# Starting layer 0's gathers on a partly built table, and moving half of its one-hots to ScalarE, in a graph network on one core

## The reference

```python
xt = jnp.einsum('ni,rio->rno', x, weight)            # 8 relations, 6250 x 256 each
messages = xt[edge_type, dst]                        # one row of 256 for each edge
out = segment_sum(messages, src, 6250)               # summed by src
x = layernorm(x + relu(out + bias))
```

## Time and profile before

| | us |
|---|---|
| median of 3 runs | 6381.3 (6370.28 to 6396.28) |
| span of the profiled execution | 6384.2 |
| edges loaded, first tiles of the table, block 0 ranked | 0 to 124 |
| slots 0 to 223 beside the rest of the table | 124 to 431 |
| sums | 431 to 2976, first add at 439.3 |
| second layer's tables | 2976 to 3100 |
| walk | 3100 to 5950 |
| final stage | 5950 to 6384 |

### The profile page before, as it was taken

The page is one execution under the profiler, slowest core; times in us unless marked ns, Lnnn a source line. Parts: engine busy times, 40 slices in busy tenths (PEclk is TensorE's granted clock), DMA queues, the critical chain, the costliest instruction groups (busy, mean ns, idle before and its releaser), DMA issues. The chain is left out here.

```text
span 6384.2 us, 87308 instructions
## 1 busy us (share of the span) xinstructions
PE 4813.9 (75%) x20011; PEld 3228.2 (51%) x20011; DVE 4590.7 (72%) x14055; ACT 2915.4 (46%) x7582; POOL 3197.8 (50%) x3370
## 2 busy tenths in 40 slices
PE   8986666666666666557777777877777777788898
PEld 4543334333333333334566665666666666666666
DVE  6977777777777777556377777777777777777766
ACT  4764444444444444002355555555555555555322
POOL 2025565555656566665255555555555555554000
PEclk9997787787777878678889988899899989889999
DMA  6432222222222222335455555555555555555100
GB/s 192 138 120 82 83 85 82 83 83 81 84 83 83 83 84 84 107 91 175 140 156 166 161 161 162 157 168 162 162 161 163 165 162 168 157 162 154 52 11 28
DMA packets 346029, 779.02 MB, mean 122 GB/s; under 512 B 75122, under 2 KB 176519, under 8 KB 345525
## 3 DMA queue, kind: packets, MB, share of 16 engines
q0 software_dynamic: 214608, 659.52, 35.5%
q1 hardware_dynamic: 127285, 111.00, 5.6%
q10 hardware_dynamic: 3632, 2.88, 0.2%
HBM read 691.52 MB, written 81.59 MB: 121 GB/s over the span
## 5 line engine op out<-in xcount | busy, mean ns | idle before, releaser
L1719 POOL DMA_INDIRECT big<-kv_table,walk_s x1664 | 1578.5, 949 | 1246.9 <-PE pb L1758 601.7
L757 POOL DMA_INDIRECT big<-xt_table,big x1617 | 1542.3, 954 | 1044.6 <-issue 504.0
L932 PE MATMUL pb<-big,walk_s 128*128 128x256 f32 x3234 | 1285.1, 494 | 457.9 <-DVE node_a L1143 200.4
L766 ACT ACTIVATE walk_s<-walk_s,big 128x128 f16<-128x128 f16 x3136 | 1076.9, 393 | 1197.4 <-DVE walk_s L1065 656.7
L1143 DVE TENSOR_TENSOR node_a<-node_a,pb 128x256 f32 (+1 forms) x1617 | 667.0, 413 | 680.2 <-remote 369.2
L1758 PE MATMUL pb<-big,early 128*128 128x264 f32 x3328 | 1000.5, 450 | 188.2 <-issue 169.9
L932 PEld LDWEIGHTS pb<-big,walk_s 128*128 128x128 f32 x3234 | 650.8, 246 | 628.5 <-issue 526.3
L1894 DVE TENSOR_TENSOR big<-big,pb 128x1024 f32<-128x1024 f32 x416 | 505.7, 1216 | 573.0 <-PE pb L1742 287.8
L1742 PE MATMUL pb<-node_a,late 128*128 x3328 | 869.7, 407 | 20.5 <-ACT late L1821 13.6
L1758 PEld LDWEIGHTS pb<-big,early 128*128 128x128 f32 x3328 | 698.3, 221 | 362.3 <-issue 223.9
L843 PE MATMUL pb<-walk_s 128*128 128x256 f16 x1568 | 501.2, 322 | 420.9 <-ACT walk_s L766 272.4
(11 more groups left out here) (313 smaller groups left out, 5743.8 us busy)
## 6 DMA issues: line engine op xcount, KB each, us to landing
xt_table<-big SPq DMA_DIRECT2D x98, 512.0 KB
big<-kv_table,walk_s POOLq DMA_INDIRECT x1664
big<-xt_table,big POOLq DMA_INDIRECT x1617
late<-pen_table SPq DMA_DIRECT2D x832, 12.1 KB
kv_table<-big SPq DMA_DIRECT2D x49, 256.0 KB
x_store<-big SPq DMA_DIRECT2D x49, 128.0 KB
big<-in_x POOLq DMA_DIRECT2D x48, 128.0 KB, 3.3
big<-x_store SPq DMA_DIRECT2D x6, 1024.0 KB, 11.9
```

The costliest lines, as they stand in the source:

```text
L757: e.indirect_dma_start(sum_rows[:, q % SUM_ROWS, k, :], None, xt_table, bass.IndirectOffsetOnAxis(ap=idx_all[:, i:i + 1], axis=0))\
L766: ins = e.activation(hot_v[:, t % SORT_HOTS, v, :], hot_q[:, t % SORT_HOTS, :], ACT.Copy, scale=part_c[:, t:t + 1])
L932: e.matmul(pb[:, bank, 0:D], one_hot, sum_rows[:, q % SUM_ROWS, k, :], start=True, stop=True)\
L1719: e.indirect_dma_start(rows[:, q % ROW_RING, k, 0:2 * D], None, kv_table, bass.IndirectOffsetOnAxis(ap=src_i[:, i:i + 1], axis=0))\
```

## The change

The rows of `xt_table` stand by node, then by relation, so that a store writes pieces of 4 KB, and the low nodes of all relations stand first in it. Since the edges come sorted by `dst`, a block's gathers touch only the tiles of its own nodes.

The l0 stage makes only products 20 to 83 (`TABLED` 84) ahead of the sums. Slots 0 to 143 (`AHEAD`) are put between products 56 and 84. The remaining 112 products run inside the sums, one after every sixth item up to item 666, in bank 1, one at a time (`product_at`); each waits until the one before it is copied out. The turns of their tiles run there too (`turn_at`). ScalarE takes the copy at the end of the same item.

GpSimd's gathers of a block wait for the stores of as many tiles as the block can touch (`tiles_for`, 19 for block 0). The remaining 80 slots of the lead are made up in items 0 to 79, which carry two slots each (`lead`). Block 1 is ranked in 54 slots as before. Blocks 2 to 12 are ranked in 126 slots each, all with the scan in PSUM. A scalar flag tells whether `dst` really is sorted and a block's last nodes lie within its tiles; if not, the kernel takes a branch that makes the whole table first, which these inputs don't take.

The one-hots of every second quad of items come from ScalarE: four activations `Abs(place - iota)` into bf16, 128 columns each, and one `Relu(1 - ...)` over 512 columns.

Three smaller things: the loads of x for tiles 7 to 48 move from GpSimd's queue to SP's; the bias copies into the sums move ahead of the slots; an iota of 128 x 1664 (`walk_iotas`, L1321) moves from the first stage to the place behind GpSimd's last gather.

```diff
-        xt_v = xt_table.rearrange("(r n) o -> n r o", r=REL)
+        xt_v = xt_table.rearrange("(n r) o -> n r o", r=REL)
+AHEAD = BT + 16
+FIRST, BEHIND, TABLED = 4 * EARLY + 36, 2, 4 * EARLY + 64
+TABLE_PACE = 6
+        def hot_by_scalar(i):
+            return i < T and i // QUAD % 2 == 1
+        def lead(i):
+            return min(AHEAD + 2 * i, PRE + i)
+        def slots_at(i):
+            return range(lead(i), lead(i + 1))
+        def product_at(i):
+            n = TABLED + i // TABLE_PACE
+            return n if i % TABLE_PACE == 0 and n < 4 * W else None
+        def tiles_for(b):
+            if b == 0:
+                return TABLED // 4 - 2
+            first = b * BT - (W - 1)
+            return min(W, (TABLED + (first - 30) // TABLE_PACE) // 4)
...
+            with e.Else():
+                e.sem_inc(s_sorted, 1)
+                for i in range(PART_ITEMS):
+                    b = block_of(i)
+                    if i == 0 or b != block_of(i - 1):
+                        e.wait_ge(s_xst[0], 16 * tiles_for(b))
+                        e.wait_ge(s_xst[1], 16 * tiles_for(b))
+                    gather(e, i, tiles_for(b))
@@ l0_scalar @@
+            for n in range(4 * EARLY, TABLED):
+                if n % 4 == 0:
+                    keep_x(e, n // 4 + 1)
+                keep_product(e, n)
...
+                for t in slots_after(n):
+                    slot(t)
+            quad_abs(QUAD)
+            for i in range(ITEMS):
+                for t in slots_at(i):
+                    slot(t)
+                if turn_at(i) is not None:
+                    keep_x(e, turn_at(i))
+                if product_at(i) is not None:
+                    keep_product(e, product_at(i))
+                if hot_by_scalar(i + 1) and (i + 1) % QUAD == 0:
+                    quad_relu((i + 1) // QUAD)
+                if hot_by_scalar(i + QUAD + 1):
+                    quad_abs(i + QUAD + 1)
@@ l0_tensor @@
             for i in range(ITEMS):
-                slot(PRE + i)
+                for t in slots_at(i):
+                    slot(t)
...
                 total(i)
+                if turn_at(i) is not None:
+                    turn_x(e, turn_at(i))
+                if product_at(i) is not None:
+                    product(e, product_at(i))
@@ l0_vector @@
             for i in range(ITEMS):
                 j = closing(i)
-                if j is None or j >= READY:
+                if not hot_by_scalar(i) and (j is None or j >= READY):
```

More of the change, by code:

```diff
@@ L527, in edges_float @@
             e.memset(raw_next[:, last], JUNK).then_inc(s_padded, 1)
+            c = Chain(e, s_dv0)
+            for b in range(PART_BLOCKS):
+                c.add(e.memset(limits[:, b:b + 1], P * tiles_for(b)))
             e.wait_ge(s_rawload, 16 * 12)
@@ L740, in table_io, with gather @@
         def table_io(e):
-            for n in range(2 * EARLY, 2 * W):
-                store_xt(e, n)
+            for w in range(EARLY, W):
+                if w + 2 < W:
+                    load_x(e, w + 2)
+                store_xt(e, 2 * w)
+                store_xt(e, 2 * w + 1)
+        def gather(e, i, tiles):
+            q, k = divmod(i, 4)
+            if i < T:
+                got.done(e, block_of(i))
+            else:
+                e.wait_ge(s_close, LISTED)
+            if k == 0 and q >= SUM_ROWS:
+                summed.done(e, (q - SUM_ROWS) * 4 + 3)
+            e.indirect_dma_start(sum_rows[:, q % SUM_ROWS, k, :], None, xt_table[0:tiles * P * REL, :],
+                                 bass.IndirectOffsetOnAxis(ap=idx_all[:, i:i + 1], axis=0))\
+                .then_inc(s_rows[q % SUM_ROWS], 16)
@@ new lines, in part_gather @@
+        def part_gather(e):
+            e.wait_ge(s_flag, 1)
+            flag = e.value_load(unsorted[0:1, 0:1], min_val=0, max_val=1)
+            with e.If(flag == 1):
+                order_move(e)
+                e.sem_inc(s_sorted, 1)
+                for i in range(PART_ITEMS):
+                    gather(e, i, W)
+            with e.Else():
+                e.sem_inc(s_sorted, 1)
+                for i in range(PART_ITEMS):
+                    b = block_of(i)
[3 more added lines that the diff above has]
+                    gather(e, i, tiles_for(b))
@@ L744, in l0_gather @@
         def l0_gather(e):
-            for w in range(EARLY + 2, W):
-                load_x(e, w)
             e.wait_ge(s_xst[0], 16 * W)
             e.wait_ge(s_xst[1], 16 * W)
[L749 to L759, removed]
+            for i in range(PART_ITEMS, ITEMS):
+                gather(e, i, W)
@@ L883, in slot @@
                     close_place()
[L884 to L885 removed]
+                for b, s in ranking(t):
+                    if b == 1 and s == 13:
                         counts(b)
[L887 removed]
+                    if s == (23 if b == 1 else 1):
                         windows(b)
[L889 removed]
+                    if s == (49 if b == 1 else 115):
                         turn_pos(b)
+                    if s == (111 if b == 1 else 121) and b + 1 < BLOCKS:
+                        counts(b + 1)
             turn_x(e, EARLY)
[L893 to L907 removed]
+            for n in range(4 * EARLY, TABLED):
+                if n % 4 == 0:
+                    turn_x(e, n // 4 + 1)
+                    e.wait_ge(s_xtc, n // 4 + 1)
+                product(e, n)
+                for t in slots_after(n - BEHIND):
+                    slot(t)
+                if n == 4 * EARLY + 7:
+                    counts(0)
+                if n == 4 * EARLY + 12:
+                    windows(0)
+                if n == 4 * EARLY + 33:
+                    turn_pos(0)
+            for n in range(TABLED - BEHIND, TABLED):
                 for t in slots_after(n):
@@ L1146, in l0_vector @@
             e.memset(x_in[:, 2, :], 0.0).then_inc(s_xz, 1)
+            c.add(e.memset(ones_p, 1.0))
             c.add(e.memset(cum_w[:, 0, :], 0.0))
```

258 lines of the change are left out of this document (161 added, 97 removed).

## The result

The changed kernel takes 6439.0 us (median of 6 runs, 6414.3 to 6470.1) against 6380.0 (6 runs, 6370.3 to 6407.3): a ratio of 1.0085, 95% interval 1.0059 to 1.011. It is slower, by more than 0.5%. I had forecast 6334, faster, with a range of 6255 to 6435; the time lies 4 us above the range and on the other side of the kernel before, where the rival of the lock step had it.

A forecast was written before the change was run, and what follows sets the result against it. Non-overlapping stages: TensorE's products and slots bound the first; in the sums no engine is full, and work plus stops set the pace. -171 + 51 + 71 + 1 = -48: 6336 on the profile, 6334 on the median, range 6255 to 6435.

The forecast's parts named there:

- the rival of the lock step: Items 80 to 672: TensorE and ScalarE wait for each other around products, pace 1.95, +213 us; time 6475, chance 0.19.
- Start of the gathers: Stage before the sums: first gather at 260, first add at 268 in place of 439.3, -171 us.
- The first 80 items: Start of the sums, two slots an item: 191 us in place of 140, +51, between +36 and +70.
- Products in items 80 to 672: Sums, a product every sixth item: 1.71 us an item against 1.59, over 592 items +71 us.
- about 1.4 us of idle TensorE with the semaphores: Sums, at each product: TensorE's next slot waits while ScalarE copies the product (0.59) and then scales that slot (0.66).
- stops: Sums: time in which several engines stand at once, of unknown cause; 0.36 us of an item's 1.59.
- the 0.36: Sums: us per item left between the modelled work of 1.23 and the pace of 1.59, added as a constant.
- ScalarE's one-hots: Sums, every second quad: 0.26 us an item more on ScalarE, expected to change nothing; 0, at most -20 us.
- 1.06 is below the pace: nothing: Sums: ScalarE's 0.70 us an item plus 0.26 for one-hots and 0.10 for copies, expected to cost no time.
- The stops shrink: Rival, sums: a gather's rows lie close together, so 0.36 us falls by a quarter, -145 us; time 6190, chance 0.05.
- The clock rule: Rival, items 80 to 672: products raise TensorE's clock to 0.89, +18 in place of +71; time 6283, chance 0.09.
- The last part: Behind the sums: the moved iota of 9.15 us hides behind waits for the adds, +1 us, +9 if uncovered.

The follow-up runs named there:

- the first experiment: The changed kernel, with ScalarE's product copies in the sums four items later (turned tiles' copies one later, their turns two later): 6288.7 us, ratio 0.9838 to the kernel before.
- Experiment 4: The changed kernel, but VectorE makes the one-hots of every quad of the sums and ScalarE none: 6352.2 us, ratio 0.9955 to the kernel before.
- experiment 5: The changed kernel with the copies four items later and all one-hots of the sums on VectorE: 6313.5 us, ratio 0.9834 to the kernel before.
- experiment 9: The changed kernel with copies four items later and the sums' products and copies cut from 512 columns to 32: 6258.3 us, ratio 0.9789 to the kernel before.
- experiments 8 and 10: Changed kernel, copies four items later, plus TensorE's slots one item later (6294.8 us, 0.9798), or instead adds two items behind, not three (6360.2 us, 0.9941).

## Why the prediction was wrong

- **Start of the gathers:** right, and by the mechanism that the sum had. First gather 255.5 for 260, first add 263.6 for 268. ScalarE is the fullest engine from 200 to 256 (53.74 of 56 us), the nineteen tiles were stored well before, and the list came last.
- **The first 80 items:** +40.7 for +51, right in kind. With the copies later they take 162.9 us in place of 180.0 (426.93 less 264.04), so some 17 us of it were already the tie.
- **Products in items 80 to 672:** this step failed, +191 for +71. The term that was mis-sized is "about 1.4 us of idle TensorE with the semaphores": TensorE stood 3.0 us behind ScalarE's scalings for each product (257.7/85), and ScalarE 4.9 us ahead of its copy, for a product of 1.72. With 3.0 in its place the forecast's own sum gives an estimate of 1.94 us for an item, where 1.92 was measured; with no such idle time it gives 1.69, as in the first experiment. That 1.94 comes out so well is in part luck, as some of the 3.0 are stops, which the 0.36 counts again. And this is what was wrong in kind: I had added the stops as a constant 0.36 to an item's work. A pause at a product was no longer shared by engines with prepared work; it held all that stood behind the copy.

The experiments show how the parts of this step hang together. These are the us from the add of item 80 to that of item 672 (944.1 in the kernel before):

| | as changed | short products and copies | all one-hots on VectorE |
|---|---|---|---|
| copy in its own item | 1135.1 | 1024.2 | 1050.1 |
| copy four items later | 1001.7 | 963.2 | 995.8 |

Taking the tie away first gives 133 us, then the products' and copies' work 38, and 19 are left unassigned. Taking the work away first gives 111 us, and the tie then 61. So the shares depend on the order: behind the tie the same work costs three times what it costs without it, and the one-hots 85 us in place of 6.

- **The rival that came true:** lock step, 6475 forecast for a span of 6468.4, decided by a pace above 1.84, measured 1.92. That the two times lie so close is partly luck: its products were to cost +213 and cost +191, and 33 us that it didn't have came in behind the sums. I had given it 0.19, and argued against it that "VectorE's own chain hides part of each". It hid what the earlier trace rows shows as slack of ScalarE behind VectorE; a wait of 4.9 us every six items uses that up. That TensorE then falls to the low clock is seen at 1005.49, but the clock in the mean rose (below), so that part of the rival isn't what costs the time.
- **ScalarE's one-hots:** "1.06 is below the pace: nothing" was wrong in this kernel, and right without the tie. All of them on VectorE saves 0.013 of the ratio, some 83 us, with the tie, and nothing that can be measured without it; from item 672 on, where there is no copy, the pace is 1.56 us in both kernels. The Trainium skill, "ScalarE: Activation LUTs", Rules for kernel authors, advises VectorE and not ScalarE for relu, max, min, add and mul. Experiment 4 agrees, where ScalarE is late; experiment 5 shows no cost where it isn't.
- **The stops shrink:** no. 1471.0 against 1477.1 us after item 672, with the rows of a gather close together.
- **The clock rule:** the granted clock did rise with the products, 0.83 against 0.79, and to between 0.85 and 0.89 in the experiments with whole products; with short ones it was 0.79 and 0.80. The Trainium skill, "TensorE: Matmul & The Clock Gate", Part 1, says that activity releases the throttle; the trace agrees in direction. The pace followed the waits and not the clock: in experiment 4 the clock is 0.89 at a pace of 1.78, in experiment 9 it is 0.80 at 1.63.
- **The last part:** +1 forecast for the iota. It takes 9.18 us at 3023.86, and the last record gathers still wait 6.53 us for the adds, so it is hidden. The +34 us of the table lie behind the sums, in unchanged code; the twelve profiles of this case have 3384 to 3429 us there. The profiled run is also 31 us above its kernel's median, while the medians are 59 us apart. I take it for the spread of single executions; no run was made for it.
- **A reading:** VectorE's share from 200 to 431 is 196.24/231, 85% and not 86%. Nothing rests on it.

What the stops are stays open. So does whether four items' delay is better than one.

The version with the copies four items later beats both kernels: 0.9838 (0.9781 to 0.9896) against the kernel before, 91 us by the medians on the same chip, where my sum for the change as written had been 48.

## What to carry to other kernels

Put an instruction that waits for another engine's long result where that result is surely there, some items later in the in-order queue, and not in the item that asks for it: what is lost isn't the wait but all prepared work queued behind it. When you cost a wait, ask which engine was ahead before and by how much; an engine whose idle time is all "behind X" is ahead of the others, and an edit that turns that into idle time behind something else makes its whole work count, the cheap parts too: here 111 us for work that costs 38 without the tie. A removed wait can come back on another engine (experiments 8 and 10), so read the waits of all engines after each edit.

## What the runs showed of the hardware that was not expected

ScalarE's copy can start long after its product has ended. In the row at 1004.26 that is 2.9 us after the product's recorded end (999.46 plus 1.88; the ends of matmuls are modelled), and the releaser of 232.8 of the 418.3 us ahead of the copies is remote. It isn't so at each product: of the 85 in the window half have their copy within 0.04 us of the end, and 37 more than 1 us behind it. VectorE and TensorE have nothing running in this pause either, from 1002.03 to 1004.26, while GpSimd issues a gather every 1.25 us, so not every engine stands in it. No run here says where such a pause comes from. I take it for the reason why slack of an item or more is worth so much in this loop, and that isn't shown.

A product's recorded time depends on the clock that TensorE comes into it with: 1.88 us at 999.46, with a granted clock of 1.00, and 3.14 at 900.22 in the first experiment, most of it at 0.50.
